# Graph attention layers on one core: the second layer loads the one-hot matrices that the first one wrote to DRAM

## The chip, the cores and the metric

The kernel runs on one core of a Trainium2 chip. The metric is the device time of one launch in microseconds (us), lower is better. A core has five instruction queues that run beside each other and meet only at semaphores: TensorE (PE in the profile; PEld is its weight load), VectorE (DVE), ScalarE (ACT), GpSimd (POOL) and SyncE (SP). The 16 DMA engines serve the queues of SP (called q1 in the profile) and of POOL (q0).

## The reference, cut to what matters

A graph of 6,250 nodes with 128 features and 100,000 edges goes through two graph attention layers of three heads (the part that the change touches), and then through a third stage of another kind. One of the first two layers computes:

```
xl = (x @ Wl + bl).reshape(n, 3, 128)
xr = (x @ Wr + br).reshape(n, 3, 128)
e = leaky_relu(xl[src] + xr[dst], 0.2)
score = einsum('ehd,hd->eh', e, att)
m = segment_max(score, dst)
ex = exp(score - m[dst])
alpha = ex / segment_sum(ex, dst)[dst]
out = segment_sum(alpha[:, :, None] * xl[src], dst) + bias
```

Edges and self loops together are 106,250. The list of edges is the same in both layers; weights and features differ.

## The kernel before, in words

The edges are sorted by destination once. Destinations are cut into 49 blocks of 128 nodes; the sorted edges fill **tiles** of 128 edges, each of one block. Two tiles are a **group** (`GS = 2`), eight groups are a **chunk** (`CG = 8`, 16 tiles). There are 464 groups, 58 chunks, and both layers go through all of them in the function `gat_edges(k, att, tag)`, which is called with tag 1 and tag 2 and does the same work both times. Its work for one group g:

- POOL gathers the 256 rows of `xl` by source index from DRAM into one of 16 slots of `ring` (two indirect DMAs of 128 rows of 390 words, `gather`, L1209).
- SP loads, for every second group, the destinations within the block of four tiles, spread over all partitions (`load_keys`, L1237, 128 KB into `lo_bc`), for every chunk the indices (`load_index`, L1228) and three sets of gates (`load_gates`, L1248 and L1252, nine DMAs).
- DVE compares (`picks`, L1390): `pick[node, edge]` is 1 where the edge's destination is this partition's node; one instruction makes the four tiles of two groups. It is the weight with which PE spreads a node's `xr` to its edges (`look`, L1270).
- DVE adds the gathered rows to what PE spread (`add`, L1405), multiplies with the attention vector (`weigh`, L1413); ACT sums each head of each tile into a score (`reduce`, L1360, six pairs of instructions a group).
- Once a chunk, a chain of some 20 small instructions on DVE, PE and ACT takes the maximum over segments, the exponential and its transpose (`turn`, `scans`, `turn_ends`, `sequence`, `carry`, `turn_carry`, `spread_fwd`, `spread_bwd`, `shift_rows`, `exps`, `turn_back`, `spread_weights`).
- The gathered rows are multiplied with their weights (`weight`): ACT does it by head and tile (L1344), four instructions in an even group and six in an odd one; in even groups DVE does the third head of both tiles in one instruction (L1427).
- DVE compares the other way round (`places`, in the helper `key_rows`, L957): `place[edge, node]`, a group's two tiles. It is the weight with which PE sums the edges into their block (`sums`, L1283); DVE adds the sum into the accumulators (`add_up`, L1452, and L1447 three times in a chunk's first group).

What sets the order is `pipeline`: each engine has a written list of (lead, function), and in its step t it calls each function for group t + lead, in the order of the list. An engine's step is one pass through that list. So in step t DVE adds group t+1, weighs t, makes places and the third head for t-11, adds up t-13, and in even steps makes picks for t+4; PE looks for t+2 and sums t-12; SP loads indices for t+12, keys for t+8. `place` and `pick` have two buffers each: the comparison waits until PE has used the buffer (`summed`, `looked`).

Of the kernel before, what the change touches and what calls it, by code (L numbers as in the profile page):

```python
# [13 lines left out]
ds = bass.ds  # L14
# [4 lines left out]
H = 3  # L19
# [43 lines left out]
WORK_W = 14200  # L63
# [75 lines left out]
class Core:  # L139


    def __init__(self, nc, ctx):
# [47 lines left out]
        self.rowgates = dram("rowgates", [2, TILES], F32)  # L190

# [959 lines left out]
def gat_edges(k, att, tag):  # L1151

    nc = k.nc
    groups, U = GROUPS, 2 * CG
# [7 lines left out]
    place = [cut(GS * P) for _ in range(2)]  # L1162
# [21 lines left out]
    index_set, lo_ready, gate_set = ([k.sem(f"a{tag}_{n}{s}") for s in range(2)] for n in ("index", "lo", "gate"))  # L1184
# [12 lines left out]
    with nc.Block() as block:  # L1197
# [18 lines left out]
        def _(sp):  # L1216
# [38 lines left out]
            pipeline(sp, groups, [(12, load_index), (8, load_keys), (0, load_gates)], U)  # L1255

        @block.tensor
        def _(pe):
            def look(j, s):
                g = U * j + s  # L1260
                if s % 2 == 0:
# [12 lines left out]
            def sums(j, s):  # L1274
                g = U * j + s
                pe.wait_ge(placed, g + 1)
                pe.wait_ge(weighted, g + 1)
                pe.wait_ge(byvec, CG * j + s // 2 + 1)
                if later(g, 2):
                    pe.wait_ge(acced, g - 1)  # L1280
                for u in range(GS):
                    at = s * W + u * HE
                    last = nc.tensor.matmul(sums_in[s % 2], place[s % 2][:, u * P:(u + 1) * P], ring[:, at:at + HE],  # L1283
                                            start=u == 0, stop=u == GS - 1)
                last.then_inc(summed, 1)
# [41 lines left out]
        def _(act):  # L1327
# [38 lines left out]
        def _(dve):  # L1366
# [16 lines left out]
            def picks(j, s):  # L1383
# [4 lines left out]
                if later(g, 4):  # L1388
                    dve.wait_ge(looked, g - 2)
                nc.vector.tensor_scalar(pick[s // 2 % 2], lo_bc[s // 2 % 2], k.part_f[:, 0:1], None, ALU.is_equal  # L1390
                                        ).then_inc(picked, 1)

            def first_lane(j, s):
                if s % CG:
                    return
                dve.wait_ge(picked, CG * j + s // 2 + 1)
# [121 lines left out]
            def spread_weights(j, s):  # L1518
                if s % CG != CG - 1:
# [11 lines left out]
            pipeline(dve, groups, [(-13, add_up), (-2, scans), (-3, shift_rows), (1, add), (-2, sequence), (-11, places),  # L1531
                                   (-2, carry), (0, weigh), (-2, spread_fwd), (-3, spread_weights), (-11, weight),
                                   (4, picks), (-2, spread_bwd), (4, first_lane)], U)
# [466 lines left out]
```

## Time and profile before

| | |
|---|---|
| median of 3 runs | 7215.49 us (7204.37, 7215.49, 7318.86) |
| the profiled execution | 7202.38 us, its span 7200.5 us |
| groups of layer 1 | about 1900 to 3520 us of the span |
| groups of layer 2 | about 3766 to 5425 us |
| busy over the span | DVE 81%, PE 71%, POOL 55%, ACT 52% |
| DMA over the span | 657.24 MB, mean 91 GB/s; HBM written 33.88 MB |
| mean granted TensorE clock | 0.874 of full speed |

How to read it: the shares over the whole span mix the sorting, two attention layers and the third stage. What the change touches is read from windows inside a layer: 2000 to 3400 us for the first and 3900 to 5300 us for the second, 1400 us each, in which the granted clock is 1.00. Busy time over such a window, divided by the groups in it, is an engine's work on one group. Instructions on an engine overlap a little, so what one of them costs is the distance from its start to the next one's start, which is less than its own duration.

### The profile page before, as it was taken

To read this page: it belongs to the slowest core of one execution; us is meant where nothing else is said; L and a number is where in the kernel's file an instruction comes from. 1 tells how busy PE (TensorE), PEld (TensorE's weight loads), DVE (VectorE), ACT (ScalarE), POOL (GpSimd) and SP (SyncE) were. 2 spreads that over 40 slices of the span, in tenths; PEclk is the share of its full clock that TensorE was granted. 3 is DMA by queue.
4 is the path that set the end of the run, shared out by engine and by line. 5 is a ranking of instruction groups with operands and counts; after the bars stand their busy time and mean duration, and the time that the engine had idled before them with its cause. 6 is when DMAs were issued, how large, how long until landed. Compare 5 with 4: busy or idle time off the path is not lost. (4 is left out here: it accounts for less than half of the span.)

```text
span 7200.5 us, 128816 instructions
## 1 busy us (share of the span) xinstructions
PE 5138.8 (71%) x22244; PEld 2877.3 (40%) x22245; DVE 5824.7 (81%) x13976; ACT 3716.2 (52%) x17417; POOL 3967.3 (55%) x3546
## 2 busy tenths in 40 slices
PE   3386589972588898988877889889885555445452
PEld 2254233321244444444443444444443344444442
DVE  9596899972599999999848999999996455555556
ACT  5142500001399999999738999999993200000000
POOL 0688868882266666656305665666650255555552
PEclk9975899985799999999989999999997776776765
DMA  0234000001355555555424555555560233333333
GB/s 12 31 66 47 6 1 1 1 3 41 113 138 139 138 140 140 140 138 139 77 71 130 139 139 139 139 138 140 139 126 21 79 95 97 96 97 97 98 96 59
DMA packets 397679, 657.24 MB, mean 91 GB/s; under 512 B 141671, under 2 KB 259365, under 8 KB 396947
## 3 DMA queue, kind: packets, MB, share of 16 engines
q0 software_dynamic: 185888, 481.62, 27.2%
q1 hardware_dynamic: 211442, 172.59, 9.9%
q14 instruction: 326, 2.66, 0.2%
q8 instruction: 23, 0.38, 0.0%
HBM read 617.73 MB, written 33.88 MB: 90 GB/s over the span
## 5 line engine op out<-in xcount | busy, mean ns | idle before, releaser
L1209 POOL DMA_INDIRECT feat_area<-xl_table,feat_area x1856 | 1984.9, 1069 | 1721.1 <-PE bank L1283 680.1
L1360 ACT ACTIVATE feat_area<-feat_area 128x130 f32<-128x130 f32 x5568 | 1642.7, 297 | 181.2 <-issue 119.3
L1270 PE MATMUL bank<-node_area,feat_area 128*128 x3712 | 1470.2, 519 | 353.8 <-DVE feat_area L1405 158.5
L1344 ACT ACTIVATE feat_area<-feat_area 128x128 f32<-128x128 f32 x4640 | 1443.0, 387 | 64.6 <-issue 64.4
L1283 PE MATMUL bank<-feat_area 128*128 128x390 f32 x3712 | 1408.5, 502 | 68.1 <-ACT feat_area L1344 21.8
L1772 POOL DMA_INDIRECT feat_area<-kv_table,feat_area x832 | 809.8, 973 | 899.7 <-DVE feat_area L1869 352.5
L600 POOL DMA_INDIRECT rec_by_dst<-feat_area,gather_col x800 | 1123.0, 1404 | 281.3 <-issue 240.1
L1360 ACT ACTIVATION_READ_ACCUMULATOR feat_area<-feat_area 128x1 f32 x5568 | 1040.0, 187 | 26.9 <-issue 26.4
L1270 PEld LDWEIGHTS bank<-node_area,feat_area 128*128 128x128 f32 x3712 | 637.4, 191 | 997.9 <-issue 732.5
L1405 DVE TENSOR_TENSOR feat_area<-bank,feat_area 128x780 f32<-128x780 f32 x928 | 886.0, 955 | 65.1 <-remote 41.0
L1283 PEld LDWEIGHTS bank<-feat_area 128*128 128x128 f32 x3712 | 666.6, 190 | 645.8 <-issue 246.3
L1810 PE MATMUL bank<-feat_area 128*128 128x136 f32 x1664 | 388.9, 403 | 714.0 <-DVE feat_area L1869 672.4
L1413 DVE SCALAR_TENSOR_TENSOR feat_area<-feat_area 128x780 f32<-128x780 f32 x928 | 886.4, 955 | 0.0
L1822 ACT ACTIVATE feat_area<-feat_area 128x32 f32<-128x32 f32 x208 | 47.7, 229 | 1370.1 <-DVE feat_area L1857 754.0
L1886 DVE TENSOR_TENSOR node_area<-node_area,bank 128x136 f32 x832 | 242.5, 291 | 506.2 <-issue 160.6
L805 PE MATMUL bank<-feat_area 125*128 125x416 f16 x3200 | 636.5, 343 | 8.3 <-DVE feat_area L765 8.3
L1810 PEld LDWEIGHTS bank<-feat_area 128*128 128x128 f32 x1664 | 332.0, 288 | 764.2 <-DVE feat_area L1869 355.8
L1452 DVE SCALAR_TENSOR_TENSOR node_area<-node_area,stays,bank 128x390 f32 x812 | 493.8, 608 | 21.1 <-PE bank L1283 20.3
L1010 ACT ACTIVATE node_area<-node_area 128x6272 f32<-128x6272 f32 x2 | 10.9, 5429 | 815.7 <-DVE node_area L976 815.7
L763 DVE TENSOR_SCALAR feat_area<-feat_area 125x128 f16<-125x128 f16 x1600 | 419.4, 346 | 0.3
L805 PEld LDWEIGHTS bank<-feat_area 125*128 125x128 f16 x3200 | 248.4, 98 | 396.6 <-DVE feat_area L765 185.7
L957 DVE TENSOR_TENSOR feat_area<-iota_f,lo_col 128x256 f32<-128x256 f32 x928 | 379.8, 409 | 0.0
(313 smaller groups left out, 6762.8 us busy)
## 6 DMA issues: line engine op xcount, KB each, us to landing
feat_area<-lo_slot SPq DMA_DIRECT2D x464, 128.0 KB
feat_area<-xl_table,feat_area POOLq DMA_INDIRECT x1856
feat_area<-lo_slot_src SPq DMA_DIRECT2D x208, 128.0 KB
node_area<-lo_edge SPq DMA_DIRECT2D x100, 256.0 KB
xl_table<-feat_area SPq DMA_DIRECT2D x98, 195.0 KB, 2.2
feat_area<-kv_table,feat_area POOLq DMA_INDIRECT x832
rec_by_dst<-feat_area,gather_col POOLq DMA_INDIRECT x800
feat_area<-gates SPq DMA_DIRECT2D x348, 32.0 KB
```

The lines of the kernel that those rows point to most:

```text
L600: pool.indirect_dma_start(k.rec_d, bass.IndirectOffsetOnAxis(ap=self.pos[:, c:c + 1], axis=0), self.pay[:, c, :], None).then_inc(self.writ ...
L805: last = nc.tensor.matmul(out[n][m], self.to_lane[s][:, n * P:(n + 1) * P], self.to_tile[s][:, m * half:(m + 1) * half], start=False, stop ...
L1209: pool.indirect_dma_start(ring[:, at:at + HE], None, k.xl, bass.IndirectOffsetOnAxis(ap=index[s // CG][:, n:n + 1], axis=0)).then_inc(gath ...
L1270: last = nc.tensor.matmul(pair[s % 2][:, u, 0:HE], pick[s // 2 % 2][:, c:c + P], k.node[:, ds(columns[0], HE)], start=True, stop=True)
L1283: last = nc.tensor.matmul(sums_in[s % 2], place[s % 2][:, u * P:(u + 1) * P], ring[:, at:at + HE], start=u == 0, stop=u == GS - 1)
L1344: last = nc.scalar.activation(row[:, 0:D], row[:, 0:D], ACT.Copy, scale=row[:, D:D + 1])
L1360: last = nc.scalar.activation(at, at, ACT.Copy, accum_out=score[s // CG][:, to:to + 1])
L1405: nc.vector.tensor_tensor(z[s % V].rearrange("p (u e) -> p u e", u=GS), pair[s % 2][:, :, 0:HE], ring[:, s * W:(s + 1) * W].rearrange("p ( ...
L1413: nc.vector.scalar_tensor_tensor(out=zu, in0=zu, scalar=0.0, in1=att_w.unsqueeze(1).to_broadcast([P, GS, HE]), op0=ALU.max, op1=ALU.mult). ...
L1452: last = nc.vector.scalar_tensor_tensor(out=k.node[:, ds(to, HE)], in0=spare, scalar=k.stays[:, ds(g, 1)], in1=sums_in[s % 2], op0=ALU.mul ...
L1772: pool.indirect_dma_start(kv[s][:, u * KV:(u + 1) * KV], None, k.kv, bass.IndirectOffsetOnAxis(ap=index[s][:, u:u + 1], axis=0)).then_inc( ...
L1810: nc.tensor.matmul(k.bank[2 + u][:, 0:VW], place[s % 2][:, u * P:(u + 1) * P], wv[s % 2][:, u * VW:(u + 1) * VW], start=True, stop=True).t ...
```

## The change

Layer 1 (`tag == 1`) computes as before, and SP writes each `pick` (256 KB for two groups, `store_picks`) and each `place` (128 KB a group, `store_places`) to two new DRAM tensors. Layer 2 (`kept`) makes neither comparison: SP loads `pick` and `place` from there (`load_picks`, `load_places`) and no longer loads the keys. `place` has four buffers in both layers. In layer 2 the third head of every group, not of every second, is weighted on DVE, so ACT has four instructions a group.

```diff
+        self.picks = dram("picks", [GROUPS // 2, P, 2 * GS * P], F32)
+        self.places = dram("places", [GROUPS, P, GS * P], F32)
...
+    kept = tag == 2
+    Q = 4
...
-    place = [cut(GS * P) for _ in range(2)]
+    place = [cut(GS * P) for _ in range(Q)]
...
-            pipeline(sp, groups, [(12, load_index), (8, load_keys), (0, load_gates)], U)
+            def store_picks(j, s):
+                if s % 2 == 0:
+                    return
+                sp.wait_ge(picked, CG * j + s // 2 + 1)
...
+            def store_places(j, s):
+                g = U * j + s
+                sp.wait_ge(placed, g + 1)
...
+            def load_picks(j, s):
+                if s % 2:
+                    return
+                g = U * j + s
+                if later(g, 4):
+                    sp.wait_ge(looked, g - 2)
...
+            def load_places(j, s):
+                g = U * j + s
+                if later(g, Q):
+                    sp.wait_ge(summed, g - Q + 1)
...
+            if kept:
+                pipeline(sp, groups, [(12, load_index), (5, load_picks), (0, load_gates), (-9, load_places)], U)
+            else:
+                pipeline(sp, groups, [(12, load_index), (8, load_keys), (3, store_picks), (0, load_gates), (-12, store_places)], U)
+                for n in range(2):
+                    sp.wait_ge(pick_moved[n], 16 * (groups // 4))
+                for n in range(Q):
+                    sp.wait_ge(place_moved[n], 16 * (groups // Q))
...
-                    for h in range(H - 1 if s % 2 == 0 else H):
+                    for h in range(H - 1 if s % 2 == 0 or kept else H):
...
                 if later(g, 4):
                     dve.wait_ge(looked, g - 2)
+                    dve.wait_ge(pick_moved[s // 2 % 2], 16 * (4 * j + s // 4))
...
-                if later(g, 2):
-                    dve.wait_ge(summed, g - 1)
-                key_rows(k, place[s % 2], k.lo_col, g * GS, GS).then_inc(placed, 1)
+                if later(g, Q):
+                    dve.wait_ge(summed, g - Q + 1)
+                    dve.wait_ge(place_moved[s % Q], 16 * (U // Q * j + s // Q))
+                key_rows(k, place[s % Q], k.lo_col, g * GS, GS).then_inc(placed, 1)
...
-                if s % 2:
+                if s % 2 and not kept:
                     return
```

DVE in the loop of layer 2, from the last scan instructions of a chunk on, before. L1472 to L1475 are `sequence`, L1483 and L1484 `carry`, L1405 and L1413 `add` and `weigh`, L957 `places`, L1390 `picks`, L1427 the third head:

```order
L1472 TENSOR_TENSOR feat_area<-feat_area 51x128
L1473 COPY feat_area<-feat_area 1x3
L1475 COPY feat_area<-bank 1x3x16
L957 ISA
L957 TENSOR_TENSOR feat_area<-iota_f,lo_col 128x256
L1483 SCALAR_TENSOR_TENSOR feat_area<-feat_area 1x51
L1484 SCALAR_TENSOR_TENSOR feat_area<-feat_area,bank 1x51
L1413 SCALAR_TENSOR_TENSOR feat_area<-feat_area 128x780
```

The same place with the change (L1470 is `weigh`, L1485 the third head):

```order
L1531 COPY feat_area<-feat_area 1x3
L1533 COPY feat_area<-bank 1x3x16
L1541 SCALAR_TENSOR_TENSOR feat_area<-feat_area 1x51
L1542 SCALAR_TENSOR_TENSOR feat_area<-feat_area,bank 1x51
L1470 SCALAR_TENSOR_TENSOR feat_area<-feat_area 128x780
```

The comparison that stood between `sequence` and `carry` is gone, and so `carry` follows directly on the instruction whose result it reads. In the steps without a chunk's chain DVE's list with the change is add_up, add, weigh, third head:

```order
L1510 SCALAR_TENSOR_TENSOR node_area<-node_area,stays,bank 128x390
L1459 REGISTER_ALU
L1462 TENSOR_TENSOR feat_area<-bank,feat_area 128x780
L1470 SCALAR_TENSOR_TENSOR feat_area<-feat_area 128x780
L1485 TENSOR_TENSOR feat_area<-feat_area 128x2x128
```

SP in the loop of layer 1 where it loads indices, before:

```order
L1228 ISA [waits a1_gathered8,a1_gathered9,a1_gathered10,a1_gathered11,a1_gathered12,a1_gathered13,a1_gathered14,a1_gathered15]
L1228 DMA feat_area<-gather_col 128x16
L1235 REGISTER_ALU
L1237 ISA [waits a1_picked]
L1237 DMA feat_area<-lo_slot 128x512
```

The same place with the change (L1234 index, L1243 keys, L1266 `store_picks`, L1273 `store_places`):

```order
L1234 ISA [waits a1_gathered0,a1_gathered1,a1_gathered2,a1_gathered3,a1_gathered4,a1_gathered5,a1_gathered6,a1_gathered7]
L1234 DMA feat_area<-gather_col 128x16
L1241 REGISTER_ALU
L1243 ISA [waits a1_picked]
L1243 DMA feat_area<-lo_slot 128x512
L1266 ISA [waits a1_picked]
L1266 DMA picks<-feat_area 128x512
L1271 REGISTER_ALU
L1273 ISA [waits a1_placed]
L1273 DMA places<-feat_area 128x256
```

The stores stand behind the wait for the gathers of a whole chunk and behind the load of keys, in SP's one queue.

## Rows read from the trace of the kernel before

**Rows 1.** Busy time of each engine inside layer 1 and inside layer 2.
```profile
core 0: us, PE busy (x) PEld busy (x) DVE busy (x) ACT busy (x) POOL busy (x), PEclk, DMA share, GB/s
2000.00:3400.00 1400.00, 1252.44 (x3648) 605.86 (x3647) 1378.92 (x2940) 1341.23 (x6990) 868.62 (x810) 1.00 0.53 139
3900.00:5300.00 1400.00, 1255.01 (x3652) 607.03 (x3651) 1380.86 (x2943) 1342.48 (x6998) 867.52 (x811) 1.00 0.53 139
```

**Rows 2.** Groups of instructions on DVE, 3900 to 5300 us.
```profile
line engine op names shapes xcount | busy us, mean ns | idle before us <-releasers
L1405 DVE TENSOR_TENSOR feat_area<-bank,feat_area 128x780 f32<-128x780 f32 x406 | 387.5, 954 | 0.9 <-DMA feat_area<-xl_table,feat_area 0.9
L957 DVE TENSOR_TENSOR feat_area<-iota_f,lo_col 128x256 f32<-128x256 f32 x406 | 166.1, 409 | 0.0
L1390 DVE TENSOR_SCALAR feat_area<-feat_area,part_f 128x512 f32<-128x512 bf16 x202 | 99.1, 491 | 0.0
L1427 DVE TENSOR_TENSOR feat_area<-feat_area 128x256 f32<-128x256 f32 x203 | 84.2, 415 | 0.0
```

**Rows 3.** The weighting on ACT, 3900 to 5300 us, same view.
```profile
L1344 ACT ACTIVATE feat_area<-feat_area 128x128 f32<-128x128 f32 x2028 | 631.8, 387 | 26.8 <-issue 26.7
```

**Rows 4.** Timeline of DVE: start us, duration us, instruction.
```profile
4501.03 0.42 DVE L957 TENSOR_TENSOR feat_area<-iota_f,lo_col 128x256 f32<-128x256 f32 x1
4501.36 0.96 DVE L1413 SCALAR_TENSOR_TENSOR feat_area<-feat_area 128x780 f32<-128x780 f32 x1
4502.24 0.42 DVE L1427 TENSOR_TENSOR feat_area<-feat_area 128x256 f32<-128x256 f32 x1
4502.58 0.61 DVE L1452 SCALAR_TENSOR_TENSOR node_area<-node_area,stays,bank 128x390 f32 x1
...
4505.20 0.48 DVE L1390 TENSOR_SCALAR feat_area<-feat_area,part_f 128x512 f32<-128x512 bf16 x1
4505.60 0.61 DVE L1452 SCALAR_TENSOR_TENSOR node_area<-node_area,stays,bank 128x390 f32 x1
```

**Rows 5.** Who waited for whom, 3900 to 5300 us: total us, times, longest.
```profile
POOL feat_area L1209 <- issue: 245.9, 579, 1.6
...
PE bank L1270 <- DVE feat_area L1405: 61.9, 82, 0.9
PE bank L1270 <- issue: 46.0, 130, 0.6
...
PE bank L1283 <- issue: 9.1, 20, 0.9
...
DVE feat_area L1528 <- DVE feat_area L1526: 8.1, 50, 0.2
```

**Rows 6.** DMA queues, 3900 to 5300 us: packets, MB, share of 16 engines.
```profile
q0 software_dynamic: 51853, 161.86, 43.3%
q1 hardware_dynamic: 41940, 32.08, 9.3%
```

**Rows 7.** Timeline around one load of indices in layer 1, SP and DVE.
```profile
2604.34 0.15 DVE L1397 COPY feat_area<-feat_area 128x1 f32<-128x1 f32 x1
...
2605.34 0.51 SPq L1228 DMA_DIRECT2D feat_area<-gather_col  x1
...
2606.19 5.26 SPq L1237 DMA_DIRECT2D feat_area<-lo_slot  x2
...
2610.40 0.48 DVE L1390 TENSOR_SCALAR feat_area<-feat_area,part_f 128x512 f32<-128x512 bf16 x1
```

**Rows 8.** DMA issues: count, KB each, median us to landing.
```profile
xl_table<-feat_area SPq DMA_DIRECT2D x98, 195.0 KB, 2.2
...
gates<-feat_area SPq DMA_DIRECT2D x1, 2048.0 KB, 6.3
```

**Rows 9.** Windows as in rows 1, near each layer's end and at its start.
```profile
3440.00:3480.00 40.00, 31.89 (x93) 15.66 (x91) 36.15 (x78) 34.17 (x178) 21.65 (x21) 0.97 0.99 135
5310.00:5350.00 40.00, 32.38 (x96) 15.94 (x95) 36.39 (x81) 32.90 (x172) 22.63 (x22) 0.97 0.93 132
...
1900.00:1910.00 10.00, 7.18 (x14) 3.77 (x15) 4.19 (x8) 0.30 (x2) 7.87 (x8) 0.64 0.71 183
```

More of the change, by code:

```diff
@@ L62 @@
 NODE_W = max((NB + 1) * HE, 2 * NPAD + NB * VW)
-WORK_W = 14200
+WORK_W = 14720
 class Order:
@@ L1183, in gat_edges @@
     gathered = [k.gather_sem(f"a{tag}_gathered{s}") for s in range(U)]
-    index_set, lo_ready, gate_set = ([k.sem(f"a{tag}_{n}{s}") for s in range(2)] for n in ("index", "lo", "gate"))
+    index_set, lo_ready, gate_set, pick_moved = ([k.sem(f"a{tag}_{n}{s}") for s in range(2)]
+                                                 for n in ("index", "lo", "gate", "pick"))
+    place_moved = [k.sem(f"a{tag}_place{s}") for s in range(Q)]
     names = ("loaded", "order", "preset", "picked", "looked", "added", "weighed", "reduced", "placed", "weighted",
@@ L1260, in look @@
                 g = U * j + s
-                if s % 2 == 0:
+                if s % 2 == 0 and kept:
+                    pe.wait_ge(pick_moved[s // 2 % 2], 16 * (4 * j + s // 4) + 16)
+                elif s % 2 == 0:
                     pe.wait_ge(picked, CG * j + s // 2 + 1)
@@ L1275, in sums @@
                 g = U * j + s
-                pe.wait_ge(placed, g + 1)
+                if kept:
+                    pe.wait_ge(place_moved[s % Q], 16 * (U // Q * j + s // Q) + 16)
+                    pe.wait_ge(byvec, g + 1)
+                else:
+                    pe.wait_ge(placed, g + 1)
+                    pe.wait_ge(byvec, CG * j + s // 2 + 1)
                 pe.wait_ge(weighted, g + 1)
-                pe.wait_ge(byvec, CG * j + s // 2 + 1)
                 if later(g, 2):
@@ L1282, in sums @@
                     at = s * W + u * HE
-                    last = nc.tensor.matmul(sums_in[s % 2], place[s % 2][:, u * P:(u + 1) * P], ring[:, at:at + HE],
+                    last = nc.tensor.matmul(sums_in[s % 2], place[s % Q][:, u * P:(u + 1) * P], ring[:, at:at + HE],
                                             start=u == 0, stop=u == GS - 1)
@@ L1395, in first_lane @@
                     return
-                dve.wait_ge(picked, CG * j + s // 2 + 1)
+                if kept:
+                    dve.wait_ge(pick_moved[s // 2 % 2], 16 * (4 * j + s // 4) + 16)
+                else:
+                    dve.wait_ge(picked, CG * j + s // 2 + 1)
                 nc.vector.tensor_copy(first[s // CG], pick[s // 2 % 2][:, 0:1]).then_inc(lane_set, 1)
@@ L1529, in spread_weights @@
                                         ).then_inc(faded, 1)
-            pipeline(dve, groups, [(-13, add_up), (-2, scans), (-3, shift_rows), (1, add), (-2, sequence), (-11, places),
-                                   (-2, carry), (0, weigh), (-2, spread_fwd), (-3, spread_weights), (-11, weight),
-                                   (4, picks), (-2, spread_bwd), (4, first_lane)], U)
+            if kept:
+                pipeline(dve, groups, [(-13, add_up), (-2, scans), (-3, shift_rows), (1, add), (-2, sequence),
+                                       (-2, carry), (0, weigh), (-2, spread_fwd), (-3, spread_weights), (-11, weight),
+                                       (-2, spread_bwd), (1, first_lane)], U)
+            else:
+                pipeline(dve, groups, [(-13, add_up), (-2, scans), (-3, shift_rows), (1, add), (-2, sequence), (-11, places),
+                                       (-2, carry), (0, weigh), (-2, spread_fwd), (-3, spread_weights), (-11, weight),
+                                       (4, picks), (-2, spread_bwd), (4, first_lane)], U)
 def load_cols(nc, sp, cols, sources, loaded):
```

13 lines of the change are left out of this document (added).

## The prediction, made before the changed kernel ran

> **What bounds the kernel now.** The page's slices give the stages; I then cut windows out of the two layers that the change touches. In both, DVE is busy 1379 and 1381 of 1400 us, ACT 1341 and 1342, PE 1252 and 1255, and POOL 868, at a granted clock of 1.00, which is the level of 2.4 GHz [rows 1]. The second window holds 406 groups, by the count of `add` and of `places` [rows 2], so a group takes 1400 / 406 = 3.448 us. Work on one group is 1380.9 / 406 = 3.401 us on DVE, 1342.5 / 406 = 3.307 on ACT and 1255.0 / 406 = 3.091 on PE. DVE is the bound by a narrow margin, ACT is 0.09 us behind it and PE 0.31. The waits agree: PE's largest one is for DVE's `add`, 61.9 us in 82 times, and DVE hardly waits for anybody [rows 5]. POOL works 867.5 / 406 = 2.14 us a group, with its own gaps ("issue", 245.9 us) 2.74 us. The DMA engines are busy 53% at 139 GB/s. So a gain can come only from layer 2, where DVE and ACT both get relief, and it ends at the next engine, which is PE.
>
> **DVE in layer 2.** Of an instruction I count the distance to the next start, since neighbours overlap. `places` costs 4501.36 - 4501.03 = 0.33 us in each group, `picks` 4505.60 - 4505.20 = 0.40 us in every second, so 0.20 a group; the third head costs 4502.58 - 4502.24 = 0.34 us and is added in every second group, 0.17 a group [rows 4]. Net 0.33 + 0.20 - 0.17 = 0.36 us less, so 3.401 - 0.36 = 3.04 us. (By full durations, from rows 2, it would be (166.1 + 99.1 - 84.2) / 406 = 0.45; that counts the overlap twice.) In one step of a chunk `carry` now follows directly on the copy it reads. Where this kernel has such a pair, DVE idles 8.1 us / 50 = 0.16 us [rows 5] in place of an overlap of about 0.08: 0.24 us a chunk, 0.03 a group. DVE: **3.07 us**.
>
> **ACT in layer 2.** 2028 instructions took 631.8 us, 0.312 us each [rows 3], five a group now and four then: 3.307 - 0.312 = **3.00 us**.
>
> **PE** does the same work: **3.09 us** by busy time. Its idle time put down to "issue" is 46.0 + 9.1 us [rows 5], 0.14 a group. If all of that is its own (registers loaded between a wait and a matmul), the floor is 3.23; if it is hidden waiting for DVE, 3.09.
>
> **The new period.** Four engines then lie at 3.09, 3.07, 3.00 and 2.74 us. Today the period is 0.047 us above the busiest engine, with the next one 0.09 behind; with three within 0.09, and a chain in each chunk in which PE, DVE and ACT answer each other in turn, I take twice that, 0.09: 3.18 us. The bounds are 3.09 (no waits) and 3.30 (PE's 3.23 and the same 0.07 to 0.09 on it). 464 groups x (3.448 - 3.18) = **-124 us**, with bounds of -166 and -69.
>
> **The transfers of layer 2.** Each group brings 256 KB more (262 kB), less the keys' 64 KB. q0 and q1 moved 193.9 MB at 52.6% of 16 engines [rows 6], which is 263 GB/s at 100%; at the start of layer 1 they moved 183 GB/s at 0.71, 258 at 100% [rows 9]. 262 kB / 3.18 us is 82 GB/s, or 0.31; gathers at the shorter period take 0.47, the rest 0.03: 0.81. It fits, at zero, if loads come in time. `load_places` for g is issued when the sum of g-4 is done, three steps or 9.5 us ahead; `load_picks` also has three steps. Behind the load of indices SP is late by some 1.5 us [rows 7]. The cover is those three steps; a load that took over 7 us would break it.
>
> **Layer 1.** DVE stays the bound and nothing is taken off it. SP gets 4 stores of picks and 8 of places a chunk. Its issues in a row lie 0.85 us apart (2605.34 to 2606.19, rows 7), so with its 14 DMAs of today it uses under 26 x 0.85 = 22 of 27.6 us. Two new waits stand on DVE before the comparisons. The tight one: behind the load of indices SP issues keys at 2606.19, the store of a pick would come 0.85 later, at 2607.04, and DVE overwrites that buffer at 2610.40 [rows 7]: 3.36 us for the store. Behind DVE's wait are queued `add_up` and the next `add`, and behind these PE and ACT. In the other steps the store has a whole two steps, about 6.9 us; `places` with four buffers has more still, so it costs nothing. A store of 195 KB landed in 2.2 us and one of 2048 KB in 6.3 [rows 8]; on the line between, 256 KB takes 2.3 us. Beside gathers that hold 43% of the engines I allow 3 to 4 us, so the stall is between 0 and 4 us a chunk (the upper end from the 6.3 us row with 1 us of SP's lateness); near the 195 KB row I take 0.2 us x 58 chunks = **+12 us**.
> The Trainium skill ("DMA: Bandwidth & Descriptors", Anatomy of one DMA) gives 2.0 us plus bytes / 436,000 per us, 2.6 us for this store, as an estimate; the same page (Latency and other measured facts) has HBM access rise from 0.2 to 2 us at high load, which would make it 4.4 us, a stall of 1.0 us a chunk and +58 us in place of +12. The trace has no store under such load, so no row decides between the two.
>
> **The ends of the layers.** For 40 us near each layer's end the DMA engines are 0.99 and 0.93 busy at only 135 and 132 GB/s, and DVE already falls to 36.2 of 40 us [rows 9]. Added traffic of about 0.3 of the engines has no room there: 0.3 x 40 = 12 us for each layer, **+24 us** (0 if gathers keep their turn, 30 if stores also slow them).
>
> **Sum.** -124 + 12 + 24 = -88 us on the profiled execution's 7202.4 us: 7114 us. That execution lies 13 us under the median of the runs shown (7215.49) and 2 us under their fastest, so I put the forecast at **7115 us**, 1.4% below the median. A measurement of this kernel tells about 2%, some 144 us, from no change.
>
> **Rivals.**
> - *Everything overlaps* (17%): the period falls to 3.10 us, -161 us, stalls and ends cost 0 to 12: 7041 to 7053 us. For it: PE's steps between chunks are free of waits once DVE is. Against it: PE's "issue" gaps and the chain in each chunk.
> - *The coupling eats it* (14%): with PE at its 3.23 us the period is 3.30, -69 + 36: 7170 us. For it: PE would be the bound, and its gaps of 0.14 us a group have no releaser in the waits.
> - *Late stores in layer 1* (13%): the pick's buffer is not free when DVE wants it, because SP's store stands behind the wait for a chunk's gathers. Price: 58 times the lateness. At 1 us 7202 - 124 + 24 + 58 = 7160; at the 2048 KB row's landing, 6.3 - 3.36 = 2.9 us, 168 us: 7270, slower than before. It cancels the gain from (124 - 24) / 58 = 1.7 us on, and reaches 2% slower only from about 4.4 us on, which needs gathers late by it as well. For it: 3.36 us of room against 2.3 us of an undisturbed store. Against it: at the 53% of today the gathers are not late, DVE waited 0.9 us for them in 1400 [rows 2].
> - The forecast itself has 56%, with its own range of 7075 to 7160.
>
> The range for all: **7040 to 7225 us**; outside are mostly the worse late stores. Faster by over 2% is below 7071: most of the first rival and a little of the forecast, 19%. Slower by over 2% is above 7360: 6%. Within 2%: 75%.
>
> **What would show it.** In a window inside layer 2: a period of 3.18 us; PE busy 97% at a clock of 1.00, DVE 96%, ACT 94%; DMA share about 0.8 at 210 GB/s; no wait of PE's `sums` or `look` for a transfer; POOL still waiting for `sums`. In layer 1: the period still 3.45 us and DVE's wait for the store under 0.3 us a chunk; 1 us or more in front of `picks` once a chunk means the late stores. Wrong would be: DVE idle before `add` for the gathers (then the DMA engines are the bound), a period of layer 1 above 3.50, or a PE that stays at 90% with waits spread over the chunk's chain.

## The result, and the profile after

The changed kernel took 7354.55 us (median of 4 runs, 7269.60 to 7376.51) beside 7226.85 us of the kernel before (4 runs on the same chip, 7204.37 to 7318.86): a ratio of 1.0176, 95% interval 1.0106 to 1.0246. The forecast was 7115 us, 1.4% faster, with a range of 7040 to 7225. The profiled execution took 7376.51 us.

That is not the whole result. All runs told of here come from seven chip sessions, and in three of them everything waits less: the kernel before took 6828 to 6847 us there and 7179 to 7366 us in the others, and the unedited change was *faster* there, 6803.43 against 6839.74 us, ratio 0.9941 (0.9924 to 0.9958). I call the sessions in which the kernel before took some 7.2 ms **A**, and those with 6.84 ms **B**; the prediction was made from, and judged in, A. Even within A the sorting ahead of the layers, which the change leaves alone, ended between 1676 and 1812 us in different runs. So I compare stages of profiles: a layer's *length* is the time from its first to its last gather issue, its *period* the distance of the `add` of group 20 to that of group 440, divided by 420.

| | layer 1, length and period | layer 2, length and period |
|---|---|---|
| before, A | 1617, 3.453 | 1616, 3.448 |
| change, A (three profiles) | 1729, 1722, 1717; 3.696, 3.673, 3.667 | 1604, 1584, 1599; 3.414, 3.370, 3.410 |
| change, B (two profiles) | 1666, 1681; 3.594, 3.633 | 1475, 1477; 3.163, 3.161 |

In the first profile layer 1 is 112 us longer and layer 2 is 12 us shorter; the sorting and the third stage, both untouched, are 49 and 22 us longer, of the 174 us between the two profiled executions.

The profiles of the two kinds differ in one more way. Each DMA raises its semaphore 16 times when its parts have landed. Of these landing signals the A profiles have 40 to 47% on record and the B profiles 88 to 91%. So in A a wait that is put down to "issue" or "remote" (to nobody in the program) can have had a releaser whose record is missing, and a time to landing is a lower bound there.

The changed kernel's windows in layer 1 and layer 2, session A; they are the counterpart of rows 1:

```profile
core 0: us, PE busy (x) PEld busy (x) DVE busy (x) ACT busy (x) POOL busy (x), PEclk, DMA share, GB/s
2000.00:3400.00 1400.00, 1175.61 (x3404) 579.30 (x3404) 1297.74 (x2746) 1257.83 (x6528) 779.42 (x750) 0.99 0.69 199
4000.00:5200.00 1200.00, 1071.36 (x3168) 546.17 (x3167) 1076.57 (x2199) 1080.16 (x5712) 735.70 (x704) 0.98 0.69 198
```

Two gathers are a group, so the second window holds 352 groups: DVE works 1076.57 / 352 = 3.06 us on one, ACT 3.07, PE 3.04. The work is what the forecast said, but each of the three engines idles a tenth of the time, where before DVE idled 1.5% [rows 1]. In session B the same stretch of layer 2 holds 380 groups:

```profile
3900.00:5100.00 1200.00, 1122.84 (x3418) 582.23 (x3417) 1154.79 (x2369) 1148.19 (x6175) 795.06 (x761) 1.00 0.73 214
```

DVE 96% busy, ACT 96%, DMA 0.73 at 214 GB/s: nearly the profile that the prediction described, but for PE, which is at 94% and not the busiest engine.

Waits of layer 1 with the change, A, 2000 to 3400 us (total us, times, longest). L1444 is `picks`, L1397 ACT's weighting:

```profile
ACT feat_area L1397 <- issue: 51.8, 22, 3.3
DVE feat_area L1444 <- DMA picks<-feat_area: 33.1, 33, 2.9
```

DVE, which waited for nobody before, waits for the store of a pick, 33 times in about 47 chunks. ACT's row had this counterpart before, in the same window:

```profile
ACT feat_area L1344 <- issue: 28.5, 25, 2.1
```

So ACT's idle time in front of its weighting, which is put down to nobody, rose from 28.5 to 51.8 us.

One chunk's load of indices with the change, SP and DVE, the place of rows 7:

```profile
2665.77 0.51 SPq L1234 DMA_DIRECT2D feat_area<-gather_col  x1
2666.87 0.68 SPq L1243 DMA_DIRECT2D feat_area<-lo_slot  x1
...
2669.02 0.01 SPq L1266 DMA_DIRECT2D picks<-feat_area  x1
...
2672.46 0.64 DVE L1444 TENSOR_SCALAR feat_area<-feat_area,part_f 128x512 f32<-128x512 bf16 x1 [1.89 <-DMA picks<-feat_area]
```

SP is held for the gathers, then issues indices, keys and, 3.25 us after the indices, the store. DVE stands 1.89 us and starts 3.44 us after the issue of the store. This chunk is one of the worst: here the store was issued 2.15 us behind the keys, while the median of the layer's 56 such places is 0.70 us, and 0.69 and 0.70 in B. From issue to the last landing on record the median pick store took 3.46 us in this profile, with about half of its landings recorded. In B, where they are all there, it took 4.1 us, in g2 (2000 to 3400 us) and in h3. I had taken 2.3, and 3 to 4 in the worst case.

```profile
picks<-feat_area SPq DMA_DIRECT2D x195, 256.0 KB, 4.1
```

Waits of layer 2 with the change, 4100 to 5100 us, in session A:

```profile
ACT feat_area L1413 <- issue: 44.5, 88, 1.2
...
DVE node_area L1510 <- PE bank L1336: 26.1, 23, 3.7
PE bank L1348 <- remote: 19.6, 9, 3.2
DVE feat_area L1462 <- DMA feat_area<-xl_table,feat_area: 17.9, 21, 2.1
```

and in session B:

```profile
ACT feat_area L1413 <- DVE feat_area L1470: 42.6, 115, 1.6
...
DVE feat_area L1462 <- DMA feat_area<-xl_table,feat_area: 19.8, 25, 1.5
...
DVE node_area L1510 <- PE bank L1336: 0.2, 1, 0.2
```

No load of picks or places is a large wait in either. The waits that differ have no releaser in the view ("issue", "remote"), and DVE's wait for the sums follows them. In A, ACT stops inside a row of twelve instructions that wait for nothing (L1413 is `reduce`):

```profile
4499.74 0.31 ACT L1413 ACTIVATE feat_area<-feat_area 128x130 f32<-128x130 f32 x1
...
4501.15 0.20 ACT L1413 ACTIVATION_READ_ACCUMULATOR feat_area<-feat_area 128x1 f32 x1 [1.09 <-issue]
...
4501.87 0.31 ACT L1413 ACTIVATE feat_area<-feat_area 128x130 f32<-128x130 f32 x1 [0.52 <-issue]
...
4502.52 0.28 PE L1348 MATMUL bank<-ident,feat_area 128*51 128x128 f32 x1 [1.65 <-ACT feat_area L1413]
```

and the chunk's chain starts late. Added up over groups 20 to 440 I call these **stops**: 55 us in the first profile of the change, 61 and 62 in the others of A, 0 in both of B, 4 in the kernel before.

Signals between engines come late in A as well. PE's sums wait for the signal of ACT's finished weighting. In layer 2 in B that signal is recorded 0.01 us after the instruction's end, in every group that has one on record (463 and 464 of 464). In the three A profiles of the change it is over 0.5 us late in 27 to 29 of some 380 recorded groups, by up to 3.7 us; in the kernel before in 6 groups, by up to 1.8 us.

### The profile page after: what moved, and what is told of

It reads as the page before. It is cut to its first block and busy times, and to the rows that moved or that the text cites. A ratio compares the mean times of both kernels' runs of the same rounds, so it can differ in the third digit from the quotient of the medians.

```text
span 7374.5 us, 132455 instructions
## 1 busy us (share of the span) xinstructions
PE 5128.6 (70%) x22244; PEld 2924.9 (40%) x22245; DVE 5682.1 (77%) x13512; ACT 3610.6 (49%) x16953; POOL 3843.2 (52%) x3546
## 5 line engine op out<-in xcount | busy, mean ns | idle before, releaser
L1215 POOL DMA_INDIRECT feat_area<-xl_table,feat_area x1856 | 1935.8, 1043 | 1872.7 <-PE bank L1336 762.9
L1413 ACT ACTIVATE feat_area<-feat_area 128x130 f32<-128x130 f32 x5568 | 1645.9, 297 | 339.5 <-DVE feat_area L1470 177.5
L1319 PE MATMUL bank<-node_area,feat_area 128*128 x3712 | 1495.3, 527 | 383.3 <-issue 237.6
L1397 ACT ACTIVATE feat_area<-feat_area 128x128 f32<-128x128 f32 x4176 | 1309.4, 387 | 74.5 <-issue 73.6
L602 POOL DMA_INDIRECT rec_by_dst<-feat_area,gather_col x800 | 1046.0, 1307 | 407.0 <-issue 239.2
L1413 ACT ACTIVATION_READ_ACCUMULATOR feat_area<-feat_area 128x1 f32 x5568 | 1041.2, 187 | 49.4 <-issue 47.9
L1319 PEld LDWEIGHTS bank<-node_area,feat_area 128*128 128x128 f32 x3712 | 656.2, 194 | 1007.2 <-issue 750.2
L1336 PEld LDWEIGHTS bank<-feat_area 128*128 128x128 f32 x3712 | 688.5, 192 | 616.3 <-issue 183.1
L1470 DVE SCALAR_TENSOR_TENSOR feat_area<-feat_area 128x780 f32<-128x780 f32 x928 | 886.9, 956 | 0.0
L1873 PEld LDWEIGHTS bank<-feat_area 128*128 128x128 f32 x1664 | 328.2, 284 | 797.7 <-DVE feat_area L1932 387.0
L303 DVE TENSOR_TENSOR node_area<-iota_b,node_area 125x512 bf16<-125x512 bf16 (+1 forms) x800 | 365.5, 514 | 0.3 <-PEq L381 0.3
```

What stands on the lines that cost most here:

```text
L602: pool.indirect_dma_start(k.rec_d, bass.IndirectOffsetOnAxis(ap=self.pos[:, c:c + 1], axis=0), self.pay[:, c, :], None).then_inc(self.writ ...
L1215: pool.indirect_dma_start(ring[:, at:at + HE], None, k.xl, bass.IndirectOffsetOnAxis(ap=index[s // CG][:, n:n + 1], axis=0)).then_inc(gath ...
L1336: last = nc.tensor.matmul(sums_in[s % 2], place[s % Q][:, u * P:(u + 1) * P], ring[:, at:at + HE], start=u == 0, stop=u == GS - 1)
L1413: last = nc.scalar.activation(at, at, ACT.Copy, accum_out=score[s // CG][:, to:to + 1])
L1470: nc.vector.scalar_tensor_tensor(out=zu, in0=zu, scalar=0.0, in1=att_w.unsqueeze(1).to_broadcast([P, GS, HE]), op0=ALU.max, op1=ALU.mult). ...
L1873: nc.tensor.matmul(k.bank[2 + u][:, 0:VW], place[s % 2][:, u * P:(u + 1) * P], wv[s % 2][:, u * VW:(u + 1) * VW], start=True, stop=True).t ...
```

## The experiments

Each stands beside the kernel before on the same chip in the same session, with one profile. A time with a ratio behind it is a median of several runs, one without is a single run. e1 to e4 ran in A, e5 to e8 in B, the four f kernels in A, the three g in B, h1 and h2 in A, h3 in B. The record gives chip number 11 to e5 to e8 and to the f kernels alike, so that number had a session of each kind. "Layer 1 3.568" is the period of layer 1 in us.

**e1: index load later** in both layers, when the gathers it waits for are long done.

```diff
-(12, load_index)
+(8, load_index)
```

> One number changed in both layers: the index load stands 8 instead of 12 groups ahead in SP's list, so SP no longer waits for a chunk's last gather before it can issue stores and loads. Theory A (SP's one queue: the store of a pick and the loads come late because they stand behind that wait): the period of layer 1 goes from 3.70 us a group back to 3.45 to 3.50, and DVE's wait before picks for the store (33 us in a 1400 us window) to under 5; layer 2 gains too, 3.41 to about 3.30. Theory B (the 200 GB/s of transfers make gathers and stores slow by themselves): layer 1 stays at 3.6 or more, layer 2 within 0.03 of 3.41. Theory C (the chain of each chunk couples PE, DVE and ACT, whatever SP does): layer 2 stays at 3.41.

7386.84 us (before 7365.73). Layer 1 3.568, half of the loss back, 58 us of its length. Behind the index load the time from the store's issue until DVE wants the buffer rose from 2.9 to 6.4 us (medians), and DVE's waits there fell from 48 us to 2. Layer 2 3.534, slower, though its stops fell to 38 us: there PE waits for the loads of places and picks (30.8 us in 18 times and 15.2 in 14, 4300 to 5500 us). SP's order matters in layer 1, but is not all of it.

**e2: layer 2 loads each buffer once** and reuses it, so its output is not the reference's. In `load_picks` (4) and `load_places` (Q):

```diff
+                if later(g, 4):
+                    return
```

> Layer 2 loads each of its two pick buffers and four place buffers once and uses them for all groups, so its output is not the reference's; layer 1 as in the changed kernel. No transfers but the gathers are left in layer 2, and no wait for them. Theory B or A (transfers or SP's queue cost layer 2 its gain): the period of layer 2 falls from 3.41 to about 3.2. Theory C (coupling of the chunk's chain): it stays at 3.35 to 3.41, and DVE still idles about 2.5 us a chunk. Layer 1 is a second sample of 3.70.

7443.26 us. Layer 2 3.447 with nearly no loads, against 3.414 with them: in A taking the loads away doesn't bring the gain back. Since the stops rose to 89 us, it does not show that the loads cost nothing.

**e3: third head as before.**

```diff
-                    for h in range(H - 1 if s % 2 == 0 or kept else H):
+                    for h in range(H - 1 if s % 2 == 0 else H):
```

> As the changed kernel, but in layer 2 DVE weights the third head of even groups only, as before, and ACT does it in odd groups. ACT's own work is then 3.31 us a group again and DVE's 2.90. If ACT's relief is worth anything, layer 2 gets slower, 3.41 to 3.5 (ACT's 3.31 plus waits). Theory C allows it to stay near 3.41 to 3.45, if the wait in each chunk and not ACT's sum of work sets the period. The third theory, that DVE's sum bounds, has it faster, 3.3.

7386.86 us. Layer 2 3.412, the same: in A moving the third head gains nothing. ACT's stops fell to 8 us and its late signals to 5 groups, but it is then the busiest engine. The edit moves a second thing: with ACT's longer list the packets of the queue that fetches instructions come back, 132 between groups 20 and 440 where the change has 8.

**e4: e1 with the chunk's chain in another order** in layer 2 on DVE and PE.

```diff
-[(-13, add_up), (-2, scans), (-3, shift_rows), (1, add), (-2, sequence),
- (-2, carry), (0, weigh), (-2, spread_fwd), (-3, spread_weights), (-11, weight),
- (-2, spread_bwd), (1, first_lane)]
+[(-13, add_up), (-3, spread_fwd), (1, add), (-3, spread_bwd), (-2, scans),
+ (-3, shift_rows), (0, weigh), (-2, sequence), (-11, weight), (-2, carry),
+ (-3, spread_weights), (1, first_lane)]
...
-[(-2, turn), (2, look), (-2, turn_ends), (-12, sums), (-2, turn_carry), (-3, turn_back)]
+[(-3, turn_carry), (2, look), (-2, turn), (-12, sums), (-2, turn_ends), (-3, turn_back)]
```

> As e1_index_lead, and in layer 2 the chunk's chain is written in another order: PE looks before it turns the scores, sums before it turns the ends, and turns the carry one step later; DVE scans after add and spreads one step later. Each answer has then half a step more time. Theory C: layer 2 falls below that of e1_index_lead by 0.1 us a group or more. Theories A and B: no change against e1_index_lead, within 0.03.

7478.69 us. Layer 2 3.541 against e1's 3.534: no gain. The wait moved: DVE now stands 60.5 us in 44 times (4150 to 5400 us) for PE's last answer of the chain, ahead of `spread_weights`, where in e1 it stood 3.7 us in 3 times (4300 to 5500 us).

**e5: stores first.** SP's list in layer 1; its two empty ScalarE instructions per group did not survive into the traced program (ACT's counts are those without them, but for one register move in a body of 16 groups), so there is no edit in layer 2 here, nor one from them in e6, e7, f3 and f4. The store of a pick also moves from lead 3 to lead 5, so it is issued two steps earlier and not only ahead of the loads.

```diff
-[(12, load_index), (8, load_keys), (3, store_picks), (0, load_gates), (-12, store_places)]
+[(5, store_picks), (-12, store_places), (12, load_index), (8, load_keys), (0, load_gates)]
```

> The change, with one edit in each layer. Layer 1: the sync engine's list of a step begins with the two stores (the store of a pick now in the step in which the pick is made), ahead of the index load that waits for gathers. Layer 2: ScalarE gets two empty instructions per group; so far its body of 16 groups was the only one without instruction packets in steady state (200 in the whole run against 326 before), and the only one whose row of reductions stops in the middle. Layer 1, measured so far 3.70 us per group: theory A (the store is issued too late, because it stands behind a wait for gathers) says 3.45 to 3.50; the rival (a store takes 3.5 us and the buffer is wanted back 3.4 us later, or write traffic slows the gathers) says 3.60 or more. Layer 2, so far 3.41: theory D (the stops in ScalarE's rows come with the missing instruction packets and cost what they last) says over 300 instruction packets in the run, under 15 us of stops against 57, and 3.25 to 3.32 us per group; its rival (the stops come with ScalarE's lighter load, or are no cause) says 3.38 or more.

6777.55 us (before 6846.18). Layer 1 3.509; the median pick store took 2.5 us. Layer 2, unedited, 3.165 with no stops: the forecast of 3.18 met by a layer that had missed it in A. Session B was found here.

**e6: no traffic.** Loads as in e2, and in layer 1 only the first four groups are stored; here too the output is not the reference's. In `store_picks` and `store_places`:

```diff
-                if s % 2 == 0:
+                if s % 2 == 0 or later(U * j + s, 4):
                     return
...
+                if later(g, Q):
+                    return
```

> The change with ScalarE's two empty instructions per group in layer 2, and with neither store nor load in steady state: layer 1 writes the first four groups' one-hots alone, layer 2 loads each buffer once and reuses it (so its sums are wrong). Layer 1: if stores are the whole loss, 3.45 us per group; if the four place buffers or their order cost something themselves, more. Layer 2: with ScalarE's stops gone (theory D) 3.13 to 3.20, since the 3 chunks of the run with single loads that had neither a stop nor a low clock took 25.0 us; if coupling of the engines alone eats the gain (theory C) 3.40 or more.

6688.27 us. Layer 1 3.442, length 1593: without stores the whole loss is gone (e8 has 1592 us), so the four buffers and the new order cost nothing. Layer 2 3.104: the loads cost 0.06 us a group in B, 28 us.

**e7: places alone** are stored and loaded; picks are compared in both layers.

```diff
-[(12, load_index), (5, load_picks), (0, load_gates), (-9, load_places)]
+[(12, load_index), (8, load_keys), (0, load_gates), (-9, load_places)]
...
-[(12, load_index), (8, load_keys), (3, store_picks), (0, load_gates), (-12, store_places)]
+[(12, load_index), (8, load_keys), (0, load_gates), (-12, store_places)]
```

> Only the places are stored and loaded; picks are compared in both layers; ScalarE's two empty instructions per group in layer 2; the sync engine's order as in the change. Layer 1: the wait in front of `picks` (0.83 us per chunk of the 2.1 us that VectorE idles) is gone by construction: 3.50 to 3.55 if the pick store is most of the loss, 3.65 if write traffic or the place stores are. Layer 2: VectorE's busy time is 24.45 us per chunk plus four pick comparisons (some 1.3 us): 3.25 to 3.35 by theory D, 3.41 or more by theory C.

6815.57 us. Layer 1 3.478 and 24 us over e6's length, so the place stores are the smaller part of the loss of 73 to 88 us. Layer 2 3.300, as expected from DVE's work.

**e8: third head alone**, on the kernel before.

```diff
-                    for h in range(H - 1 if s % 2 == 0 else H):
+                    for h in range(H - 1 if s % 2 == 0 or tag == 2 else H):
```

> The kernel before, with one edit: in layer 2 VectorE weights the third head of every group. Nothing is stored or loaded. VectorE is the bound before (97% busy), and gets four weightings of 0.42 us per chunk more: 3.45 + 0.21 = 3.65 us per group in layer 2 by addition, nothing in layer 1. Theory D expects instruction packets to fall from 326 to about 200 here too, and stops of over 20 us in ScalarE's rows of layer 2 though there is no transfer; if the stops come from transfers or from loads, there are under 10 us.

6908.75 us. Layer 2 3.589, +0.15 over its own layer 1 instead of +0.21: overlap again, 4 x 0.34 = 1.4 us a chunk is 0.17. Instruction packets fell to 195, as predicted, but there were no stops: the stops don't follow from a short body alone. Its layer 1 is the kernel before's in B: 1592 us, 3.441.

**f1 to f4: the change, stores first alone, empty instructions alone, both**, 3 rounds on one chip.

> The changed kernel itself, unedited, beside three variants of it and the kernel before on one chip. So far it was profiled on one chip only, and the last four kernels ran on another, where the third stage takes 1100 us instead of 1400 and ScalarE's rows of reductions have no stops at all (so theory D, which tied the stops to instruction packets, has fallen: two empty instructions per group left the packets at 200, and the stops were gone in all four). Theory E: stops, low clock and part of the stores' delay belong to the chip and its memory, not to the kernel. If this chip is of the second kind, it says layer 1 3.50 to 3.60 and layer 2 3.15 to 3.20 us per group, no stops, and a total 1 to 3% below the kernel before. If it is of the first kind, 3.70 and 3.41 again, with stops of some 60 us, and 1 to 2% above.

> The change with the stores at the head of the sync engine's list in layer 1 and nothing else. Theory A (late stores are the loss in layer 1): layer 1 falls by 0.1 to 0.2 us per group against the unedited change on this chip, 45 to 90 us in all, and layer 2 stays. Rival (store latency or write traffic): under 0.05.

> The change with two empty instructions per group in ScalarE's list of layer 2 and nothing else. Theory E: no effect, both layers and the total within 0.5% of the unedited change. Its rival (empty instructions take away the stops, by timing if not by instruction packets): layer 2 falls by over 0.1 us per group, where the unedited change has stops.

> Both edits: the version that took 6777.55 us beside 6846.18 of the kernel before on the other chip. Expected 1 to 2% under the kernel before on a chip like that one; on one like the first, layer 1 near 3.55 and layer 2 near 3.41, and within 1% of the kernel before.

Session A. f1 7330.05 us, ratio to before 1.0192 (1.0108 to 1.0276); f2 7257.00, 1.0046 (0.9993 to 1.0099); f3, the same program as f1 in effect, 7338.75, 1.0197; f4, the same as f2, 7276.32, 1.0089 (1.0053 to 1.0125). Layer 1's length is 1722 in f1 and 1669 in f2, 53 us less; layer 2 stays (3.370 and 3.388). f2's waits in layer 1:

```profile
ACT feat_area L1397 <- issue: 53.5, 24, 3.4
DVE feat_area L1554 <- PE bank L1364: 34.2, 21, 3.1
```

DVE no longer waits for a store. What is left has ACT's wait at L1397: it stands once in 16 groups, at the turn of ACT's loop, and some 4 us after it DVE's L1554 (`spread_fwd`) waits for the chain. The edit moved the store ahead of the loads and two steps earlier, and no run parts the two.

**g1: more code.** One real one-column ScalarE instruction per group in layer 2.

```diff
+                if kept:
+                    nc.scalar.activation(scrap[:, s:s + 1], k.part_f[:, 0:1], ACT.Copy)
```

> The change with one real, tiny ScalarE instruction (one column) per group in layer 2, 16 per body; the empty instructions of e5 to e7 and f3 turned out not to be in the traced program (ScalarE's counts are those without them), so they had tested nothing. Layer 2 of the unedited change: 199 to 200 instruction packets in the run, 57 us of stops in ScalarE's rows, 3.37 to 3.41 us per group. Theory D (the stops belong to a body that is kept and not fetched again): over 300 packets, under 15 us of stops, a wait of some 2 us at the turn of the loop as in layer 1, and 3.25 to 3.35. Theory E (the stops belong to what disturbs this chip at the time, and ScalarE's load is no cause): stops as before or, if the chip is quiet, none in either kernel, and the period within 0.05 of the unedited change.

Session B. 6841.38 us, ratio 1.0007 (0.9998 to 1.0017). The queue that fetches instructions (packets, MB, share) in the window 3900 to 5100 us, first g1, then the unedited change (h3):

```profile
q14 instruction: 117, 0.96, 0.2%
```

```profile
q14 instruction: 8, 0.07, 0.0%
```

and g1's wait at the turn, 4100 to 5100 us (L1395 is the added line):

```profile
ACT feat_area L1395 <- issue: 35.2, 19, 2.7
```

Sixteen instructions bring back instruction packets and a wait of 1.85 us at each turn of ACT's loop, where the change has none, and the period goes from 3.163 to 3.251, 41 us, the added instructions' own time among it. So a part of layer 2's gain in B came from a shorter body of ACT's loop, which nobody had planned. Whether the short body has a part in the stops in A is not settled. g1 had no session A; but in A layer 2 had 38 to 89 us of stops in every kernel with the short body, and 8 us in e3 and 4 in the kernel before, which have the long one. e3 also gave ACT more work, and in B the short body had no stops.

**g2: the change unedited.**

> The changed kernel unedited, a third profile. If the kernel before takes about 6850 us beside it, as beside e5 to e8, theory E says layer 1 3.50 to 3.60, layer 2 3.15 to 3.20 and no stops; if it takes about 7200 us, 3.67 to 3.70, 3.37 to 3.41 and 50 to 60 us of stops.

6792.48 us beside 6834.74. Layer 1 3.594 (stated: 3.50 to 3.60), layer 2 3.163, no stops.

**g3: g1 with the stores first.**

> The edit of g1 in layer 2 and the stores first in layer 1. Layer 1 as with the stores first alone, 3.55 to 3.57 us per group where the kernel before takes about 7200. Layer 2 as g1. If theory D holds this is the best version, 0 to 1% under the kernel before; by theory E it stands with the version with the stores first alone, 0.5% above.

6786.32 us, ratio 0.9928 (0.9911 to 0.9944); layer 1 3.496, layer 2 3.253.

**h1 to h3: the change unedited (h1, h3) and stores first (h2), timed.**

> The changed kernel unedited, timed. In the last session (kernel before at 6828 to 6847 us) one run of it took 6792 us: layer 2 at 3.163 us per group, layer 1 at 3.594. Theory E (the change's effect depends on what the session does to waits): a ratio of 0.992 to 0.997 if the kernel before takes about 6840 us here, 1.01 to 1.03 if it takes about 7200. Its rival (6792 was one lucky run): a ratio of 1.00 or more in either.

> The change with the stores first in layer 1, timed. From one run of e5, whose program is the same (6777.55 beside 6846.18): a ratio of 0.987 to 0.993 where the kernel before takes about 6840 us, and 1.00 to 1.01 where it takes about 7200, as f2 had.

> The changed kernel unedited, timed once more, since the last session was again of the kind in which the kernel before takes about 7200 us. Theory E: a ratio of 0.992 to 0.997 if the kernel before takes about 6840 us here, 1.01 to 1.03 if it takes about 7200. Its rival (the one run at 6792 was luck): 1.00 or more in either.

h1 and h2 in A: 7305.01 us, ratio 1.0135 (1.0090 to 1.0181), and 7239.32, 1.0038 (0.9995 to 1.0081). h3 in B: 6803.43, ratio 0.9941 (0.9924 to 0.9958). The sign turns with the session. The fastest version in B is e5, the stores first, with one run (6777.55 beside 6846.18), close to g3's 0.9928; in A no version beats the kernel before.

## Why the prediction was wrong

Two steps failed, each by some 100 us in A: the cost of the stores in layer 1, and the new period of layer 2.

**Layer 1, "I take 0.2 us x 58 chunks = +12 us": the step that failed first.** Layer 1 became 100 to 112 us longer in A and 73 to 88 in B (1666 and 1681 less e8's 1592 us). The mechanism was named, as a rival at 13%: the pick's buffer is not free when DVE wants it. Of the two numbers in it the room was right and the store's own time was not. Behind the index load the store was issued 0.7 to 0.8 us behind the keys (forecast 0.85), and DVE wanted the buffer 2.8 to 2.9 us after that in A and 3.3 in B (forecast 3.36). But the store took 4.1 us, not 2.3. DVE's waits there add up to 42 to 52 us in five profiles, 0.75 to 0.93 us a chunk in place of 0.2. The 195 KB row [rows 8] was a store of another stage, with idle queues; the margin should have come from the worse row. Where the store stands ahead of the loads, it took 2.5 us (e5) and 2.4 (g3); why it takes 4.1 right behind a load of keys is not shown. The Trainium skill ("DMA: Bandwidth & Descriptors", Anatomy of one DMA) makes it 2.6 us by its fit for GpSimd's path, while this store goes by SP's queue, and 4.4 by the same page's access time at high load (Latency and other measured facts), both as estimates; the measured 4.1 lies between, near the second, at a DMA share of 0.70. Issuing the store sooner took DVE's waits for it away and gave back 53 us (f2).

**Not in the prediction at all: stores lengthen ACT's turn of the loop.** The mean idle time of ACT there, once in 16 groups, is 1.12 us before, 1.10 without stores (e6), and 2.25 with the change, 2.17 with the stores first. 29 turns x 1.1 us would be 32 us of the 52 that f2 still loses, if each is paid in full, which no run shows. The cause of the wait is shown as far as that it comes with instruction packets (g1) and grows with store traffic (e6 against e5: 1.10 and 1.96). Of layer 1's 112 us, the store's 53 and at most 32 are told by these two causes; the rest stays open. The Trainium skill ("Runtime: NRT & Kernel Launch", Instruction fetch mechanics) says that a taken branch whose target is out of the engine's window forces a DMA fetch; the trace agrees as far as the packets go, with 109 in 1200 us of layer 2 before and 10 with the change's shorter body.

**Layer 2, "the new period ... 3.18 us" = -124 us.** In B the number was met: 3.163, and 1592 - 1476 = 116 us (against e8's layer 1, since no profile of the kernel before exists in B and its two layers are equal in A). In part that was luck, as the parts below show. In A it was 3.37 to 3.41, a gain of 12 to 32 us. By parts: DVE's work 3.06 (forecast 3.07), ACT's 3.07 (3.00), PE's 3.04 (3.09), and in B 3.04, 3.02 and 2.95. So in B the busiest engine was DVE at 3.04, where I had PE as the bound at 3.09; the period stood 0.12 above it, not 0.09; and the transfers, put at zero, cost 0.06 of that (28 us, e6). The errors nearly cancel. What failed in A is the price of coupling, "twice that, 0.09": the period stood 0.30 to 0.34 us above the 3.07 of the busiest engine, with the stops and late signals shown above. The kernel before had only 4 us of stops, so the change brought them with it as well. That with three engines at 3.04 to 3.07 nobody can make up for a stop, where before ACT and PE had 0.09 and 0.31 us a group to spare, is argued and not shown. 10 of 52 chunks in the first profile had neither stop nor low clock; they took 26.2 us, 3.28 a group, against 27.3 in the mean and 25.3 in B. So the chunks with stops or low clock hold about half of what A lost; the rest is not settled.

The clock is part of it. After a long wait in A, PE's next matmuls run at the lower level:

```profile
4609.67 1.75 PE L1336 MATMUL bank<-feat_area 128*128 128x390 f32 x4 [3.50 <-remote]
...
4611.53 2.95 PE L1319 MATMUL bank<-node_area,feat_area 128*128 x4
```

Four of these take 1.57 us at full clock. PE's sequencer passed its wait 0.03 us after ACT's signal of a finished weighting: that instruction had ended at 4605.98, and its signal is recorded at 4609.44, 3.46 us later. The granted clock was at half, 1.2 GHz, for 72 us of this layer between groups 20 and 440, in 19 stretches, nearly all right after PE had idled 1.5 to 4.8 us, and never in either layer of the kernel before. That is 36 us of full clock given away, and 17 and 29 us in the other two profiles.

**The ends, +24.** From group 440 on, layer 1 took 95.4 us instead of 83.7 and layer 2 90.6 instead of 84.1, some 13 us beside the change of period. Within its bounds of 0 to 30.

**The median and the sign.** Sum in A by what was measured: 112 - 12 = +100 us of the layers in the first profile and +73 and +83 in the others, 1.0 to 1.4% (ratios 1.0176, 1.0192, 1.0135; stages that the change leaves alone differ between runs by as much as the rest); in B (73 to 88) - 116 = -28 to -43, and -36 measured.

What the sessions differ in shows also in the third stage, which no kernel here changes. Waits of DVE, 5900 to 6400 us, in the kernel before in A, and then in e8 in B, where all else of the stage is the same code:

```profile
DVE node_area L1886 <- issue: 63.1, 31, 2.9
DVE node_area L1886 <- remote: 50.2, 30, 2.6
```

```profile
DVE feat_area L1844 <- DMA feat_area<-kv_table,feat_area: 135.6, 95, 2.2
DVE node_area L1886 <- issue: 2.9, 18, 0.2
```

In A DVE stands up to 3 us with no releaser in the view, before an instruction that in the program waits for PE's sums; in B it doesn't, and the stage takes 1098 instead of 1404 us. Why a session is of one kind or the other stays open, and so does whether the recording itself, which loses signals in A, has a part in it. The gathers' own time can't be compared: their median to the last recorded landing in layer 2 of the change was 3.45 us in A, a lower bound, and 3.88 in B.

## What to carry to other kernels

Before a wait is put on the engine that is the bound, take the room from the issue in the queue as it will stand behind its held neighbours, and the transfer's own time under the new traffic (here 4.1 us, not the 2.3 of an idle queue); where the room is less than the worse row, put the store ahead of the held transfer and issue it as soon as its data is there. When relief brings three engines within 2% of each other, little slack is left to make up for a stop: give a range that reaches to no gain, and time the change in more than one session. Before a wait is called one without a releaser, see what share of the signals the trace holds. Look at the instruction queue and at the idle time at an engine's loop turn: both move when a body grows by a few instructions or when traffic is added.

## What the runs showed of the hardware that was not expected

- A ScalarE loop body with 285 recorded instructions in 16 groups had hardly any instruction packets (10 in 1200 us) and, in B, no wait at its turn; one with 300 or 301 had 109 to 117 and waited 1.0 to 1.2 us per turn, 1.8 to 2.25 beside the stores or loads.
- Empty ScalarE instructions did not reach the traced program: two a group left one register move in a body of 16 groups.
- The same 256 KB store took a median of 4.1 us from issue to landing right behind a load of keys (g2, h3) and 2.5 us when it was issued two steps earlier and ahead of the loads (e5).
- The same program on the same code took 5% more or less by session, with stops inside rows of ACT instructions that wait for nothing (55 to 62 us in layer 2, 0 in B) and signals between engines up to 3.7 us late (0.01 in B). Its profiles held 40 to 47% of the landing signals in the slower sessions and 88 to 91% in the faster.
